# Layer 1's row sums moved to the end of their head with inverses through memory, and layer 0 worked by halves of the tokens, in a two-layer transformer kernel

## The reference

```python
# layer 0, attention: linear, 16 heads of 8
q = elu(q) + 1.0; k = elu(k) + 1.0
kv = einsum('bhnd,bhne->bhde', k, v); ksum = sum(k, axis=2)
z = 1.0 / (einsum('bhnd,bhd->bhn', q, ksum) + EPS_ATTN)
attn_out = einsum('bhnd,bhde->bhne', q, kv) * z[..., None]
x = x + attn_out @ proj_w.T + proj_b
h = gelu(layer_norm(x) @ fc1_w.T + fc1_b) @ fc2_w.T + fc2_b
# layer 1, attention: softmax, 16 heads of 64, distance bias per head
att = einsum('bhid,bhjd->bhij', q, k) / DIM_HEAD ** 0.5 + alibi_bias(S, N_HEADS)
p = softmax(att, axis=-1)
out = einsum('bhij,bhjd->bhid', p, v)      # then all heads @ Wo
```

## Time and profile before

| | |
|---|---|
| time, median of 3 runs | 2314.11 us (2312.39 to 2315.57) |
| the profiled execution: time, span | 2305.89 us, 2304.0 us |
| mean granted clock of TensorE | 0.985 of full |
| TensorE (PE) busy | 2197.2 us, 95% |
| VectorE (DVE) busy | 1829.4 us, 79% |
| GpSimd (POOL) busy | 1385.3 us, 60% |
| ScalarE (ACT) busy | 1234.0 us, 54% |

### The profile page before, as it was taken

One profiled execution on the slowest core, in us unless ns is written; L12 is line 12 of the kernel. 1 busy time (PEld: TensorE's weight loads), 2 busy tenths in 40 slices (PEclk: granted clock), 3 DMA queues, 4 the chain that ended last, 5 costly groups with the idle time before them and its releaser, 6 DMA issues. The chain is left out here.

```text
span 2304.0 us, 40435 instructions
## 1 busy us (share of the span) xinstructions
PE 2197.2 (95%) x10494; PEld 1381.0 (60%) x10531; DVE 1829.4 (79%) x4804; ACT 1234.0 (54%) x1664; POOL 1385.3 (60%) x751
## 2 busy tenths in 40 slices
PE   7989998899999999999999999999999999989995
PEld 4656665456565565656556565655556564449884
DVE  7788886788888888888888888888888887765555
ACT  2232323466666566666656666666666664444442
POOL 2112120578787787878778787887878787643331
PEclk9999999999999999999999999999999999999997
DMA  7050202000000100000100000010000000311114
GB/s 241 22 197 1 85 8 96 21 19 14 16 13 16 35 16 14 13 18 17 34 13 13 21 14 16 13 34 17 14 16 13 20 9 8 148 46 48 46 45 135
DMA packets 90230, 91.25 MB, mean 40 GB/s; under 512 B 22212, under 2 KB 74948, under 8 KB 90120
## 3 DMA queue, kind: packets, MB, share of 16 engines
q1 hardware_dynamic: 85800, 81.35, 11.4%
q0 software_dynamic: 4352, 8.99, 1.2%
HBM read 57.37 MB, written 36.33 MB: 41 GB/s over the span
## 5 line engine op out<-in xcount | busy, mean ns | idle before, releaser
L1624 ACT ACTIVATE big<-P 128x1024 f32<-128x1024 f32 x512 | 512.1, 1020 | 109.2 <-PE P L1993 85.5
L2007 PE MATMUL P<-big,V 128*64 128x512 f32 x2048 | 468.8, 599 | 1.0 <-ACT big L1630 1.0
L649 POOL TENSOR_TENSOR spair<-spair,big 128x1024 f32<-128x1024 f32 x192 | 457.4, 2382 | 15.9 <-DVE hp L810 1.3
L649 POOL TENSOR_TENSOR opair<-opair,big 128x1024 f32<-128x1024 f32 x192 | 457.3, 2382 | 15.0
L1031 DVE CUSTOM_DVE_ANT_0 big<-P,near 128x512 f32<-128x512 f32 x512 | 348.8, 681 | 112.2 <-PE P L1977 108.4
L1977 PE MATMUL P<-kq 96*128 96x512 f32 x1008 | 415.5, 433 | 14.2 <-DVE kq L1015 11.1
L1992 PE MATMUL P<-kq 97*128 97x512 f32 x1024 | 411.4, 402 | 5.7 <-issue 2.8
L1034 DVE TENSOR_REDUCE mhalf<-P 128x1 f32<-128x512 f32 x512 | 349.2, 682 | 79.0 <-PE P L1977 68.5
L1993 PE MATMUL P<-kq 128*128 128x512 f32 x1024 | 408.9, 399 | 0.0
L1977 PEld LDWEIGHTS P<-kq 96*128 96x128 f32 x1008 | 181.8, 190 | 214.3 <-issue 114.0
L2007 PEld LDWEIGHTS P<-big,V 128*64 128x64 f32 x2048 | 135.2, 136 | 265.0 <-issue 262.7
(11 more groups left out here) (316 smaller groups left out, 3663.1 us busy)
## 6 DMA issues: line engine op xcount, KB each, us to landing
slots<-later SPq DMA_DIRECT2D x4, 4224.0 KB, 15.5
kq<-auxrows SPq DMA_DIRECT2D x64, 128.0 KB, 2.3
big<-in_wex SPq DMA_DIRECT2D x8, 768.0 KB, 11.4
xt<-slots SPq DMA_DIRECT2D x76, 66.0 KB, 1.8
near<-in_aux SPq DMA_DIRECT2D x64, 64.0 KB, 1.8
big<-yrows SPq DMA_DIRECT2D x8, 512.0 KB, 7.2
wqk_hi<-wparts SPq DMA_DIRECT2D x62, 64.0 KB, 1.8
wqk_lo<-wparts SPq DMA_DIRECT2D x62, 64.0 KB, 1.9
```

The source lines that it names most:

```text
L649: pool.tensor_tensor(psum8[s][:, :], psum8[s][:, :], pfull[:, j % RING, :], ALU.add).then_inc(S["p_added"], 1)
L1624: act.activation(pfull[:, j, :], banks(2 * (j % 2)), ACT.Exp, scale=DH1 ** -0.5).then_inc(S["exp_done"], 1)
L2007: mm = pe.matmul(P[64 * i:64 * i + 64, 4, :], V1[:, j, s, :], half(pfull[:, j, :], i), start=(j == 0), stop=(j == T - 1))
```

## The change

In layer 1:

- `sum_head(s, n)` moves from the middle of head n + 1 to the end of head n, behind the last `weigh`. It waits for `q_lo` and `k_lo` of head n + 2's second halves (they use the same bank), and for the last add. Only the sum of head 0 keeps its old place.
- The four reciprocals of 128 columns are replaced. SyncE copies one row of the sums of each half into `rec`, 128 x 8; VectorE inverts these eight columns (`invert_rows`, behind bias 3 of head n + 1); SyncE writes them to memory and, when they are there, reads them back broadcast over 64 partitions each. Only the last two heads keep `invert`.
- On GpSimd `scaled_out` of head n - 1 moves behind all seven adds of head n.
- On ScalarE the copy of the sums moves to the start of the next head, and the first half of `turned_out` from the end of a head to between exponentials 0 and 1, one head later; the second half follows exponential 1.
- On TensorE the output projection's halves move behind maximum products (3, 0) and (4, 0), VectorE's additions of them behind bias 4 and behind maxima (5, 0), and the waits of `project_qk` for bank 5 follow.

In layer 0:

- The first half of hT goes to ScalarE and the second to VectorE. k and v are projected by halves of the tokens, k before v in each, and k's steps, q's steps and the products of k and v wait for halves. The copy of v moves to ScalarE.
- fc1 runs the four chunks of the first half and then those of the second; fc2's first four tiles wait for the first half only.
- The three instructions that add the projected attention to x move from VectorE to GpSimd (`x1_to_x`).
- Some `keep_busy` counts are cut (6 to 2, 6 to 2, 5 to 4, 4 to 1), the second norm of a sequence is ordered otherwise, and some semaphores are merged.

The diff, cut:

```diff
@@ -460,6 +463,21 @@
+            def invert_sums(n, s):
+
+                at = (lambda v: v) if isinstance(n, int) else sp.snap
+                sp.wait_ge(S["s_copied"], at(n + 1))
+                sp.sem_inc(G["passed"], 1)
+                for i in range(NHALF):
+                    sp.dma_start(rec[64 * i:64 * i + 64, :], sinv[s][64 * i:64 * i + 1, :].rearrange("o (c e) -> o c e", e=N // 128)).then_inc(S["r_in"], 16)
+                sp.wait_ge(S["r_inv"], at(n + 1))
+                sp.sem_inc(G["passed"], 1)
+                sp.dma_start(invd[s].rearrange("i (c e) -> (i c) e", e=N // 128), rec[:, :]).then_inc(S["r_out"], 16)
+                sp.wait_ge(S["r_out"], at(16 * n + 16))
+                sp.sem_inc(G["passed"], 1)
+                for i in range(NHALF):
+                    sp.dma_start(sinv[s][64 * i:64 * i + 64, :], invd[s, i].partition_broadcast(64)).then_inc(S["s_inv"], S_IN)
+
...
@@ -509,6 +527,8 @@
+                if behind:
+                    invert_sums(at(2 * p - 1), 1)
...
@@ -524,6 +544,7 @@
+                invert_sums(at(2 * p), 0)
...
@@ -631,14 +653,12 @@
-                pool.wait_ge(S["s_inv"], (n + 1) * NINV)
+                pool.wait_ge(S["s_inv"], (n + 1) * NHALF * S_IN)
...
-                    if behind and j == T - 2:
-                        scaled_out(1 - s, n - 1)
...
@@ -647,6 +667,18 @@
+                if behind:
+                    scaled_out(1 - s, n - 1)
+
+            def x1_to_x(b):
+
+                x1b, tens = tok(A[:, 7, :]), [128, T, D]
+                pool.wait_ge(S["x1_done"], EACH["x1_done"] * (b + 1))
+                pool.tensor_tensor(x1b, tok(A[:, 6, :]), over(biasb[:, 1, :], tens), ALU.add).then_inc(S["x1_bias"], 1)
+                pool.wait_ge(S["x1_bias"], b + 1)
+                pool.tensor_tensor(x1b, x1b, over(modg[:, b, 0, :], tens), ALU.mult).then_inc(S["x1_scaled"], 1)
+                pool.wait_ge(S["x1_scaled"], b + 1)
+                pool.tensor_tensor(tok(xs[:, b, :]), tok(xs[:, b, :]), x1b, ALU.add).then_inc(S["x_ready"], 1)
...
@@ -715,15 +748,13 @@
-                add_head(1, 2 * p + 1, True, range(1, T - 2))
-                scaled_out(0, 2 * p)
+                add_head(1, 2 * p + 1)
...
-                add_head(1, 2 * p + 1, False, range(T - 2, T))
...
@@ -997,12 +1028,19 @@
+            def invert_rows(n):
+
+                dve.wait_ge(S["r_in"], NHALF * 16 * (n + 1))
+                if not isinstance(n, int):
+                    dve.sem_inc(G["passed"], 1)
+                dve.reciprocal(rec[:, :], rec[:, :]).then_inc(S["r_inv"], 1)
+
...
-                dve.reciprocal(sinv[s][:, cols], sinv[s][:, cols]).then_inc(S["s_inv"], 1)
+                dve.reciprocal(sinv[s][:, cols], sinv[s][:, cols]).then_inc(S["s_inv"], NHALF * S_IN // NINV)
...
@@ -1067,22 +1105,21 @@
-                maxima((1, 1))
-                if out:
-                    add_out(p - 1, 0)
-                maxima((2, 0))
+                maxima((1, 1), (2, 0))
...
+                if behind == 2:
+                    invert_rows(n - 1)
...
-                    add_out(p - 1, 1)
+                    add_out(p - 1, 0)
...
-                if behind:
-                    invert(o, n - 1, 0)
+                if out:
+                    add_out(p - 1, 1)
...
@@ -1090,19 +1127,15 @@
-                if behind:
-                    invert(o, n - 1, 1)
...
-                if behind:
-                    invert(o, n - 1, 2)
+                if behind == 1:
+                    invert_rows(n - 1)
...
-                if behind:
-                    invert(o, n - 1, 3)
...
@@ -1120,20 +1153,38 @@
+
+                kpsum = tiles(2)
+                def k_min(i):
+                    ts = slice(i * TPH, (i + 1) * TPH)
+                    dve.wait_ge(S["k0_mm"], EACH["k0_mm"] * b + 2 * i + 1)
+                    dve.tensor_scalar(tok(A[:, 2, :])[:, ts, :], kpsum[:, ts, :], 0.0, None, ALU.min).then_inc(S["k0_min"], 1)
+
+                def k_done(i):
+                    ts = slice(i * TPH, (i + 1) * TPH)
+                    dve.wait_ge(S["k0_exp"], EACH["k0_exp"] * b + i + 1)
+                    dve.scalar_tensor_tensor(tok(A[:, 2, :])[:, ts, :], kpsum[:, ts, :], 0.0, tok(A[:, 3, :])[:, ts, :], ALU.max, ALU.add).then_inc(S["k0_done"], 1)
+
+                def q_min(i):
+                    dve.wait_ge(S["q0_mm"], EACH["q0_mm"] * b + i + 1)
+                    dve.tensor_scalar(half(A[:, 0, :], i), P[:, i, :], 0.0, None, ALU.min).then_inc(S["q0_min"], 1)
+
+                def q_done(i):
+                    dve.wait_ge(S["q0_exp"], EACH["q0_exp"] * b + i + 1)
+                    dve.scalar_tensor_tensor(half(A[:, 0, :], i), P[:, i, :], 0.0, half(A[:, 1, :], i), ALU.max, ALU.add).then_inc(S["q0_done"], 1)
+
+                k_min(0)
+                if b > 0:
...
-
-                kpsum = P[:, 2:6, :].rearrange("p a (t c) -> p (a t) c", c=2 * D)
-                dve.wait_ge(S["k0_mm"], EACH["k0_mm"] * (b + 1))
-                dve.tensor_scalar(tok(A[:, 2, :]), kpsum[:, :, 0:D], 0.0, None, ALU.min).then_inc(S["k0_min"], 1)
-                dve.tensor_copy(v0x[:, :, 0:D], kpsum[:, :, D:2 * D]).then_inc(S["v0_copied"], 1)
-                dve.wait_ge(S["k0_exp"], b + 1)
-                dve.scalar_tensor_tensor(tok(A[:, 2, :]), kpsum[:, :, 0:D], 0.0, tok(A[:, 3, :]), ALU.max, ALU.add).then_inc(S["k0_done"], 1)
-                dve.wait_ge(S["q0_mm"], EACH["q0_mm"] * (b + 1))
-                dve.tensor_scalar(A[:, 0, :], banks(0), 0.0, None, ALU.min).then_inc(S["q0_min"], 1)
+                k_min(1)
+                k_done(0)
+                k_done(1)
+                q_min(0)
+                q_min(1)
...
-                dve.wait_ge(S["q0_exp"], b + 1)
-                dve.scalar_tensor_tensor(A[:, 0, :], banks(0), 0.0, A[:, 1, :], ALU.max, ALU.add).then_inc(S["q0_done"], 1)
+                q_done(0)
+                q_done(1)
...
@@ -1170,13 +1221,6 @@
-                dve.tensor_tensor(tok(A[:, 7, :]), tok(A[:, 6, :]), over(biasb[:, 1, :], tens), ALU.add).then_inc(S["x1_bias"], 1)
-
-                dve.wait_ge(S["x1_bias"], b + 1)
-                dve.wait_ge(S["mod_in"], 1)
-                dve.tensor_tensor(tok(A[:, 7, :]), tok(A[:, 7, :]), over(modg[:, b, 0, :], tens), ALU.mult).then_inc(S["x1_scaled"], 1)
-                dve.wait_ge(S["x1_scaled"], b + 1)
-                dve.tensor_tensor(x[:, :, :], x[:, :, :], tok(A[:, 7, :]), ALU.add).then_inc(S["x_ready"], 1)
...
@@ -1637,7 +1680,11 @@
+                if behind == 2:
+                    sums(o, n - 1)
...
+                if behind == 2:
+                    turned_out(s, n - 2, p - 1, 0)
...
@@ -1663,20 +1710,24 @@
-                if ahead == 2:
...
-                if behind:
-                    turned_out(o, n - 1, p - 1 if s == 0 else p, 0)
...
-                act.wait_ge(S["k0_min"], b + 1)
-                act.activation(A[:, 3, :], A[:, 2, :], ACT.Exp).then_inc(S["k0_exp"], 1)
-                act.wait_ge(S["q0_min"], b + 1)
-                act.activation(A[:, 1, :], A[:, 0, :], ACT.Exp).then_inc(S["q0_exp"], 1)
+                for i in range(NHALF):
+                    act.wait_ge(S["k0_min"], EACH["k0_min"] * b + i + 1)
+                    act.activation(half(A[:, 3, :], i), half(A[:, 2, :], i), ACT.Exp).then_inc(S["k0_exp"], 1)
+                    act.wait_ge(S["k0_mm"], EACH["k0_mm"] * b + 2 * i + 2)
+                    if b == 0 and i == 0:
+                        act.wait_ge(S["v0_ones"], 1)
+                    ts = slice(i * TPH, (i + 1) * TPH)
+                    act.activation(v0x[:, ts, 0:D], tiles(4)[:, ts, :], ACT.Copy).then_inc(S["v0_copied"], 1)
+                for i in range(NHALF):
+                    act.wait_ge(S["q0_min"], EACH["q0_min"] * b + i + 1)
+                    act.activation(half(A[:, 1, :], i), half(A[:, 0, :], i), ACT.Exp).then_inc(S["q0_exp"], 1)
...
@@ -1933,10 +1985,11 @@
-                    if not isinstance(n, int) or n > 2:
-                        pe.wait_ge(S["s_copied"], n - 2)
-                    elif n == 2:
-                        pe.wait_ge(S["v_in"], 2)
+                        pe.wait_ge(S["v_in"], n)
+                    elif isinstance(n, int) and n == 3:
+                        pe.wait_ge(S["s_copied"], 1)
+                    else:
+                        pe.wait_ge(S["x_added"], n - 3 + X_AT)
...
@@ -2041,35 +2094,26 @@
-                if out:
-                    if ahead:
-                        pe.wait_ge(S["q_lo"], 2 * n + 4)
-                        pe.wait_ge(S["k_lo"], 2 * n + 4)
-                    else:
-                        pe.wait_ge(S["s_copied"], n - 1)
-                    out_proj(p - 1, 0)
...
-                    out_proj(p - 1, 1)
+                    pe.wait_ge(S["s_copied"], n)
+                    out_proj(p - 1, 0)
...
+                if out:
+                    out_proj(p - 1, 1)
...
-                if behind:
-                    if s == 0:
```

(76 more changed lines are left out.)

50 lines of the change are left out of this document (27 added, 23 removed).

## The result

| | before | changed |
|---|---|---|
| time, median of 4 runs each | 2313.47 us | 2581.48 us |
| ratio | | 1.115, 95% interval 1.1132 to 1.1169 |
| profiled execution, span | 2304.0 us | 2579.9 us |
| layer 0, up to the first transposed maxima | 400.4 us | 413.4 us |
| from there to those of the last head | 1508.3 us | 1749.6 us |

The changed kernel is slower by 268 us. Of the 275.9 us between the two profiled spans, 241.3 lie in the loop over the heads, 13.0 in layer 0, 3.6 before the last sum and 18.0 behind it. In the changed kernel the lines are others: L1040 is L1078, L1049 is L1087, L1015 is L1053, L649 is L669, L636 is L658, L1977 is L2030, L2007 is L2060, L2014 is L2067, L810 is L841. In the kernels of the experiments the lines shift again by a few; the tiles name them.

The account below looks back on a forecast made before the run. TensorE's queue was taken to set the length. 184 us for the new wait before the sum, +3 for head 1 and the last two, -11 for layer 0 made +176, so 2490 us against the median 2314.11; range 2330 to 2520.

Parts of the forecast that it names:

- the mechanism, its place and its size in even heads: Layer 1, head's end: GpSimd's adds block VectorE's combination of maxima, q_lo comes late, TensorE waits; period 26.7 us, not 23.4.
- near H+19.7 in odd heads: When the combination of maxima comes due in odd heads, H being the start of a head's first maximum product.
- the three waits of odd heads: Layer 1: scores 2 and 3 behind later exponentials (0.3 and 0.5 us), second output product behind its bank's addition (0.55).
- -11 forecast: Layer 0 in all: earlier k chain and MLP product against slower additions on GpSimd, a gain of 11 us, bounds -18 and -5.
- VectorE's own two-input instructions of the previous batch are caught: Layer 0: cost expected from moving three additions and scalings to GpSimd, where each takes some 2.4 us for 1.22 on VectorE.
- some 1.6: Layer 0: with halves of the activation, the second MLP product can begin this many us earlier.
- +176: Whole kernel: forecast slowdown in us, 184 for the new wait, 3 for head 1 and the last two, -11 for layer 0.
- Gain 0.3 us a head: Layer 1: the sum moved behind the weighing products saves this, 19 us over 62 heads, if nothing else waits.
- today's events: Kernel before: TensorE's waits for VectorE's low parts of q, 11 us in 7 of 62 heads, taken off the new wait's price.
- Rival 1: Layer 1: adds do not block the combination of maxima; periods 23.55 and 24.5 us, +17, 2331 us; chance 0.08.
- Rivals 2 and 3: Whole kernel: faster, 2273 us (2265 to 2300), chance 0.14; or nothing comes of it, transfers and waits eating the gains, chance 0.03.
- Rival 4: Layer 1: transfers of the inverses take 3 us a leg, not 1.7, and hold bias 4; +60 us; chance within the main 0.75.

Follow-up runs that it names:

- the run with the reduction: Changed kernel, with the maxima combined by a reduction over one SBUF input instead of an operation on two: 2390.98 us, ratio 1.0324.
- the run with the later turns: Changed kernel with one-input maxima, x's additions on VectorE, earlier output additions, outputs turned behind exponentials 1 and 2, second output product behind scores 5: 2283.27 us, ratio 0.9937.

## Why the prediction was right and wrong

**Right: the mechanism, its place and its size in even heads.** GpSimd's lost window, two VectorE instructions at the first boundary, the wait for add 7 and for scaled_out, q_lo behind them, and TensorE's new wait stand in the profile as written. L1078 comes due 18.3 us behind an even head's start (1110.35 less 1092.04), as forecast; an even head takes 26.5 us for a forecast of 26.7, and the run with one input takes the loss away. The transfers cost nothing, though the one back took 2.8 us instead of the 1.7 reckoned.

**Wrong: "near H+19.7 in odd heads", and then one period for all.** The prediction saw the three waits of odd heads (exponentials, bank) but let them vanish under the wait for GpSimd, with GpSimd's end fixed at H+23.8. They do not vanish. A wait ahead of the scores delays the exponentials, and in the changed kernel GpSimd waited 1.11 us for one of them in the middle of its adds; the bank held TensorE for 0.49 and 0.80 us more. In the odd head shown L1078 came due at H+21.5 and GpSimd ended at H+25.3. Odd heads took 28.57 us on average, 1.9 more than the 26.7 of the sum; with 30 such heads that is 56 us, the largest part of what is missing. The waits were sized too small as well: with nothing held on VectorE the prediction had 24.5 for odd heads, and the run with the reduction, at full clock, 25.83.

**Left out: TensorE's clock.** The prediction had no term for it, and it is part of these 56 us. In the changed kernel the granted clock falls behind the wait before the sum of nearly every even head, to 0.50, the lower of the two levels, and the odd head that follows pays. Rows of stretches of the changed kernel: us from and to, its length, busy us of TensorE, its weight loads, VectorE, ScalarE and GpSimd, the granted clock, then transfers.

```profile
1228.00:1230.00 2.00, 1.85 (x4) 0.30 (x4) 0.02 (x1) 0.00 (x0) 0.00 (x0) 0.50 0.00 0
...
1007.87:1036.15 28.28, 25.14 (x106) 15.06 (x107) 20.24 (x44) 14.80 (x18) 17.86 (x8) 0.94 0.06 17
...
1722.83:1750.69 27.86, 24.40 (x107) 13.78 (x107) 20.39 (x44) 14.79 (x18) 19.05 (x9) 1.00 0.06 17
```

The second and third are whole odd heads. The mean is 0.94 in those of 28.3 us, 0.89 or 0.90 in those of 29.5 to 29.7, and 1.00 in two of the 30 only, which are the shortest, 27.86 and 27.84 us. Both follow an even head unlike the rest (24.74 and 27.14 us), so what they give is an estimate: without the lower clock the odd heads would take 27.85, so the clock is 0.7 of the 1.9 us, some 21 us in 30 heads, and the later chain 1.15, some 35 us. The kernel before was not free of it: from its first sum to its last the granted clock was 1.00 in all heads but two, those with the two longest of its seven waits. In layer 0 the first products of the MLP paid again.

**Wrong: the sign of layer 0, -11 forecast, +13 measured.** The failed term is "VectorE's own two-input instructions of the previous batch are caught". It named the wrong victim. GpSimd's three instructions met the norm of the same batch, on the way to the MLP, with one SBUF input, and 5.5 us a batch were lost there against the 2.4 gained in the attention stage (211.93 to 234.03 for 204.48 to 228.98 before). The gain of "some 1.6" in the MLP was 1.0 at equal clock (7.49 for 8.48), and none in the changed kernel, where the clock was low. These 24 us are the second part of what is missing; with the 56 they make 80 of the 92 us between +176 and +268, and the rest isn't assigned.

**Right: the sum's place, seen late.** "Gain 0.3 us a head" can't be read where anything is held: in the run with the reduction an even head takes 23.24, but there the sum still waits 0.13 us for the last add. In the run with the later turns, where it doesn't, an even head takes 23.11 against 23.41, which is 0.30, and the sum takes 0.96 us to the next product for the 0.89 forecast.

**Small slips.** The 11 us of today's events, taken off the price, were about 15 with their restarts and the clock. And the bounds: against the median 2314.11 the prediction's own terms give 2417 to 2528, where it writes 2405 to 2525, and the range given ends at 2520, below either upper end. The 2581 us measured lie outside all of them.

**The rivals.** Rival 1 (no blocking, 23.55 and 24.5) came to be in the run with the reduction, with 23.24 and 25.83; its mean of 24.5 is half a microsecond above the 24.0 reckoned. Rivals 2 and 3 are refuted by the time. Rival 4 is refuted by the idle time before L1036, 0.0 us: VectorE never waited for a transfer there, and GpSimd once, 6.1 us.

## What to carry to other kernels

Ask of every instruction that is moved to GpSimd, and of every idle window of GpSimd that is closed, which VectorE instructions will run beside it: in these runs an operation on two SBUF tiles, or a norm from SBUF to SBUF, waited for all that was left of a GpSimd addition or product of SBUF tiles, and 0.16 us became 2.2. Where it can't be moved, see whether a reduction says the same. A wait that is "covered" by a longer one in the same head must be followed to the engines that feed the longer one, since it moves their start.

## What was not expected of the hardware

- Behind the wait before the sum of an even head, 3.2 us as a rule, the granted clock was 0.50 for some us in 28 of 30 odd heads. Behind one of 1.42 us (the head of 27.86 us) and one of 2.50 us (that of 27.84) it stayed at 1.00; in the kernel before it fell behind waits of 2.08 and 1.87 us and stayed behind five of 1.22 to 1.84. So the length of the wait alone doesn't decide it. The odd heads' times come in series (28.37, 28.65, 28.98, 29.51, then 28.27 again; 13 of 30 lie at 28.26 to 28.30), and what sets them the runs don't show.
- At a boundary between two GpSimd instructions without a gap, one held VectorE instruction passes (number 3 above) and the next is held again, in the even and the odd head shown (the four end at 1115.5 and 1089.0, both with scaled_out).
- VectorE's and ScalarE's unnamed waits at the end of the program came and went with the set of runs, or its chip, and not with the kernel. In the changed kernel's first profile they are 24 us of the two engines, and the stretch was 20 us longer (376.2 for 356.1).
